# Routing sums in the second attention: GpSimd adds the two halves of each expert's products, VectorE sums 64 values in place of 128

## The chip, the cores and the metric

One core of one Trainium2 chip runs the whole network as one program. The metric is the device time of one execution in microseconds, the median of several runs.

## The reference

Two layers work on 64 x 64 tokens of 128 values (4096 tokens, 32 units of 128 tokens). Each layer has an attention over the tokens' own sequence and a context, and then a feed-forward part made of experts. What matters here is the second attention and the router of the second experts:

```python
normed = hidden_states * jax.lax.rsqrt(var + 1e-08) * norm_weight
flat = normed.reshape(-1, d)
probs = jax.nn.sigmoid(flat @ router_w.T)        # 8 experts
scores, idx = jax.lax.top_k(probs, TOPK)         # TOPK = 2
```

The product `flat @ router_w.T` is, for each token and each of the 8 experts, a sum of 128 products. The hidden states are the residual after the second attention.

## The kernel before

The program has four stages, one behind the other: `attention0` (to about 260 us), `experts`, `attention1` (from about 700 to 1180 us) and `sorted_experts`. The residual `x` stays in SBUF, 32 units of 128 tokens by 128 values.

`attention1` is a pipeline written out by hand. Each engine runs `for n in ticks` over 46 ticks, and in each tick it works on parts of several units that are at different steps: in tick n TensorE computes the scores of unit n, the values times probabilities of unit n - 2, the queries and keys of later pairs and the output projection of an earlier pair. The order within a tick is fixed on each engine by the list of calls at the end of its block, and all order between engines is by semaphores (`tally` objects, whose `at(k)` is the count after k steps).

Four units make a group. When the attention's output of a group has been normalised (`normalise_y`, L1752, VectorE), scaled and shifted by GpSimd (`scale_y`, L1302 and L1304) and added to the residual by VectorE (`add_up`, L1761), the routing of that group may start. The first five groups of eight (ROUTED = 5) are routed inside this stage, between the attention's own work, by `route_on_pool`, `route_on_act` and `route_on_dve`. `group_at(n, k)` is the group that is at its k-th routing tick in tick n; a group's routing starts every four ticks, and lasts eleven, so two or three groups overlap.

- In routing ticks 0 to 3 GpSimd multiplies one unit each (`multiply`, L1309): the unit's 128 values times the router's weights of each of the 8 experts, 8 x 128 products for each token, into one of two buffers `prod` (the profile calls them c_work, because they lie in a work tile).
- In routing ticks 2 and 4 VectorE sums two units each (`reduce`, L1796): 8 sums of 128 for each token into `raw`. `multiply(m)` waits until `reduce(m - 2)` is done, since it writes the same buffer.
- Then come logits (L1804 to L1807), the exponential on ScalarE, probabilities (L1812), a comparison of all experts with each other on GpSimd (L1317), ranks (L1820 to L1822), positions by TensorE, the choice of two (L1841), a payload that ScalarE fills (L1454) and eight scatters (L1324) that GpSimd issues.

The steps of the attention that the prediction speaks of: VectorE writes the low part of the normed and turned input (`x_lower`, L1661, c_x_lo), which TensorE's `values` of the next tick waits for; it copies the values out of PSUM (L1669, c_v); its reciprocal of the softmax sums (L1710) lets GpSimd scale the probabilities (L1292); ScalarE copies the turned probabilities out of PSUM (L1413, c_probT). GpSimd's order in a tick is `scale_y`, `scale` twice, `route_on_pool`, `split_context` (L1281 and L1284). VectorE's is the softmax's clip (L1683) and subtraction (L1690), `route_on_dve`, L1717, `add_up`, `normalise_y`, the sums (L1697), L1661 and so on.

Of the kernel before, what the change touches and what calls it, by code (L numbers as in the profile page):

```python
# [29 lines left out]
ALU = mybir.AluOpType  # L30
ACT = mybir.ActivationFunctionType
AX = mybir.AxisListType

P = 128
B, N, C = 64, 64, 128
UNITS = B * N // P
GROUP = 4
# [1056 lines left out]
def attention1(nc, earlier, x, stats, ident, a, route, dest_rows):  # L1094
# [8 lines left out]
    with stage(nc, earlier) as ctx:  # L1103
        def sb(name, shape, dt=F32):
            return ctx.enter_context(nc.sbuf_tensor("c_" + name, shape, dt))
# [4 lines left out]
        def sem(name):  # L1110
            return ctx.sem("c_" + name)

        def tally(name):
            return Tally(ctx, "c_" + name)
# [33 lines left out]
        prod = work[:, :].rearrange("p (s e c) -> p s e c", s=2, e=E)  # L1148
# [5 lines left out]
        raw, logit, expo = (sb(n, [P, GROUP, E]) for n in ("raw", "logit", "expo"))  # L1154
# [45 lines left out]
        for cc in range(CC):  # L1200
# [5 lines left out]
        tables = ((rw[:, :, :], a["d_rw_wide"]), (norm_wide, a["d_norm_wide"]),  # L1206
                  (sums_raw, a["sums"].rearrange("p n f -> p (n f)")), (route.before[:, :, :], a["before"]),
                  (route.first_row[:, :], a["first_row"]), (route.ids[:, :, :], a["ids"]))
        tables_in, rw_made, rw_summed, r_step, scattered = (sem(n) for n in ("tables_in", "rw_made", "rw_summed", "r_step",
                                                                             "scattered"))  # L1210
        r_var_done, r_root_done, r_scaled = tally("r_var"), tally("r_root"), tally("r_scaled")
        multiplied, reduced, logit_done, expo_done = (tally(n) for n in ("multiplied", "reduced", "logit", "expo"))
        prob_done, compared, masked, pos_done = (tally(n) for n in ("prob", "compared", "masked", "pos"))
# [55 lines left out]
        def _(pool):  # L1269
# [36 lines left out]
            def multiply(m):  # L1306
                pool.wait_ge(added_up.sem, added_up.at(m // GROUP + 1))
                pool.wait_ge(reduced.sem, reduced.at(m - 1))
                pool.tensor_tensor(prod[:, m % 2, :, :], x[:, m, :].unsqueeze(1).to_broadcast([P, E, C]), rw[:, :, :],  # L1309
                                   ALU.mult).then_inc(multiplied.sem, 1)  # L1310

            def compare(g):
                by_j = both[:, 0, :, :].unsqueeze(2).to_broadcast([P, GROUP, E, E])
# [13 lines left out]
            def route_on_pool(n):  # L1327
                if n == 0:
                    pool.wait_ge(tables_in, 16 * len(tables))
                    pool.tensor_tensor(rw[:, :, :], rw[:, :, :], norm_wide.unsqueeze(1).to_broadcast([P, E, C]), ALU.mult  # L1330
                                       ).then_inc(rw_made, 1)
                    pool.tensor_tensor(route.sums[:, :, :].rearrange("p n f -> p (n f)"), sums_raw,
                                       zero[:, 0:1].to_broadcast([P, 2 * P]), ALU.subtract).then_inc(rw_made, 1)
                    pool.wait_ge(rw_made, 2)
                    weights.wait(pool, len(jobs))
                for j in range(GROUP):
                    g = group_at(n, j)
                    if g is not None:
                        multiply(GROUP * g + j)
                g = group_at(n, 5)  # L1340
                if g is not None:
                    compare(g)
                for j, (lo, hi) in enumerate(((0, 3), (3, 6), (6, 2 * GROUP))):
                    g = group_at(n, 8 + j)
                    if g is not None:
                        scatter(g, lo, hi)
# [300 lines left out]
        def _(dve):  # L1647
# [145 lines left out]

            def reduce(m):
                dve.wait_ge(multiplied.sem, multiplied.at(m + 1))
                dve.tensor_reduce(raw[:, m % GROUP, :], prod[:, m % 2, :, :], AX.X, ALU.add).then_inc(reduced.sem, 1)  # L1796

            def logits(g):
                per_row = lambda t: t[:, g % 2, :].unsqueeze(2).to_broadcast([P, GROUP, E])
# [57 lines left out]
            def route_on_dve(n):  # L1857
                if n == 4:
                    dve.wait_ge(rw_made, 2)
                    dve.tensor_reduce(rw_sum[:, :], rw[:, :, :], AX.X, ALU.add).then_inc(rw_summed, 1)  # L1860
                g = group_at(n, 8)
                if g is not None:
                    place(g)
                g = group_at(n, 7)
                if g is not None:
                    pick(g)
                g = group_at(n, 6)
                if g is not None:
                    choose(g)
                g = group_at(n, 5)  # L1870
                if g is not None:
                    probabilities(g)
                g = group_at(n, 4)
                if g is not None:
                    reduce(GROUP * g + 2)
                    reduce(GROUP * g + 3)
                    logits(g)
                g = group_at(n, 2)
                if g is not None:
                    scales(g)  # L1880
                    reduce(GROUP * g)
                    reduce(GROUP * g + 1)
# [615 lines left out]
def program(nc, a, rows, gates, planes, out):  # L2498
    with ExitStack() as ctx:
        earlier = Earlier()  # L2500
        x = ctx.enter_context(nc.sbuf_tensor("x_resid", [P, UNITS, C], F32))
        stats = ctx.enter_context(nc.sbuf_tensor("x_stats", [P, UNITS, 6], F32))
        ident = ctx.enter_context(nc.sbuf_tensor("identity", [P, P], F32))
        headmask = ctx.enter_context(nc.sbuf_tensor("headmask", [P, FOUR], F32))
        attention0(nc, earlier, x, stats, ident, headmask, a["x"], a["a_wqkvT"], a["a_wprojT"], a["a_bproj"],
                   a["a_ctx_kT"], a["a_ctx_v"], a, rows)
        experts(nc, earlier, x, stats, ident, a, gates)
        route = Routing(nc, ctx)
        attention1(nc, earlier, x, stats, ident, a, route, rows)
        sorted_experts(nc, earlier, x, stats, ident, a, rows, planes, out, route)  # L2510
        with nc.Block() as block:
            @block.sync
            def _(sp):
                earlier.clear(sp)
        earlier.replace([], ExitStack())
# [79 lines left out]
```

## Time and profile before

| | |
|---|---|
| median of 3 runs | 1485.86 us (1478.29, 1485.86, 1489.66) |
| profiled execution | 1490.25 us, span 1488.4 us |
| granted TensorE clock, mean | 0.936 |
| TensorE busy | 1255.5 us, 84% |
| VectorE busy | 1056.2 us, 71% |
| ScalarE busy | 897.0 us, 60% |
| GpSimd busy | 650.9 us, 44% |

Busy time is a sum over stages with different limits, so it doesn't say what an edit in one stage is worth. An operation that stands because another engine holds what it needs is shown as busy for all that time. The end of idle time before an instruction is put down to the engine and line that released it ("<-"). "issue" is time in which the engine waited for nothing that the profile shows.

### The profile page before, as it was taken

The numbers are of one execution on the slowest core, as the hardware profiler recorded it, in microseconds if no ns is written. First come the engines' busy times: TensorE is split into PE (matmuls) and PEld (weight loads), VectorE is DVE, ScalarE is ACT, GpSimd is POOL, SyncE is SP. The second block draws the span as 40 slices with busy tenths as digits, with TensorE's granted clock in tenths as the row PEclk, the third lists the DMA queues.
The fourth block names the chain that finished last, engine by engine and source line by source line (L and its number), as shares of the span: only waits on it lengthen the run. The fifth ranks groups of instructions, "written<-read, shape, count | busy, mean of one in ns | idle before, by whom it ended". The sixth has DMA issues, their size and how long they took to land. (4 is left out here: it accounts for less than half of the span.)

```text
span 1488.4 us, 35941 instructions
## 1 busy us (share of the span) xinstructions
PE 1255.5 (84%) x13401; PEld 1043.8 (70%) x13401; DVE 1056.2 (71%) x2080; ACT 897.0 (60%) x1699; POOL 650.9 (44%) x677
## 2 busy tenths in 40 slices
PE   4999998399999999995799999998995269998970
PEld 3777776277777777783798888887885157786750
DVE  5888887576777677764456688898896377676652
ACT  3888887566666666654455565655653258777740
POOL 3222222155555555564423345566563335165551
PEclk9999999599999999997899999999999659999985
DMA  4222221333221322131200000000000122156626
GB/s 141 92 92 94 95 97 52 120 88 91 74 65 50 91 74 65 50 93 58 84 16 10 16 10 16 11 21 27 10 12 16 52 72 78 36 168 210 219 96 182
DMA packets 88373, 109.64 MB, mean 74 GB/s; under 512 B 13322, under 2 KB 55050, under 8 KB 88202
## 3 DMA queue, kind: packets, MB, share of 16 engines
q1 hardware_dynamic: 83210, 97.05, 20.8%
q0 software_dynamic: 4992, 10.30, 2.1%
q8 instruction: 109, 1.79, 0.5%
q14 instruction: 62, 0.51, 0.1%
HBM read 61.70 MB, written 29.82 MB: 61 GB/s over the span
## 5 line engine op out<-in xcount | busy, mean ns | idle before, releaser
L828 POOL TENSOR_TENSOR b_h_lo<-b_h,b_h_hi 128x512 fp32r<-128x512 f32 x168 | 216.5, 1293 | 179.0 <-ACT b_h_hi L852 178.6
L847 ACT ACTIVATE b_zg<-b_zg 128x512 f32<-128x512 f32 x168 | 97.7, 581 | 82.2 <-PE b_zg L892 81.8
L852 ACT ACTIVATE b_h_hi<-b_h 128x512 fp32r<-128x512 f32 x168 | 105.1, 626 | 65.3 <-DVE b_h L1057 65.3
L2171 POOL DMA_INDIRECT planes_dram<-d_y_out,d_back x92 | 93.8, 1020 | 110.8 <-DVE d_y_out L2474 85.3
L1057 DVE TENSOR_TENSOR b_h<-b_zg,b_uw 128x512 f32<-128x512 f32 x168 | 116.2, 692 | 32.0 <-ACT b_zg L847 26.7
L1050 DVE TENSOR_TENSOR b_uw<-b_zu,b_gw 128x512 f32<-128x512 f32 x128 | 88.2, 689 | 57.2 <-PE b_zu L892 51.0
L2443 DVE TENSOR_TENSOR d_h_lo<-d_h,d_h_hi 128x512 fp32r<-128x512 f32 x124 | 85.4, 695 | 53.0 <-ACT d_h_hi L2208 33.1
L312 POOL TENSOR_TENSOR a_qx<-a_qT,headmask 128x256 f32<-128x256 f32 x64 | 37.9, 612 | 149.1 <-ACT a_qT L347 149.1
L1292 POOL TENSOR_TENSOR c_prob<-c_prob,c_recip 128x512 f32<-128x512 f32 x64 | 65.5, 1044 | 59.8 <-DVE c_recip L1710 59.8
L519 DVE TENSOR_REDUCE a_top<-a_score_ps 128x8 f32<-128x1024 f32 x64 | 78.1, 1220 | 18.5 <-PE a_score_ps L410 18.5
L1717 DVE TENSOR_TENSOR c_oT_lo<-c_oy,c_oT_hi 128x512 fp32r<-128x512 f32 x64 | 43.7, 683 | 55.9 <-ACT c_oT_hi L1420 55.5
L1493 PE MATMUL c_p<-c_c_hi,c_wk_hi 128*128 128x256 f32 x256 | 76.8, 300 | 5.2 <-ACT c_qx L1385 4.4
L523 DVE TENSOR_TENSOR a_prob<-a_score_ps,a_top 128x1024 f32<-128x1024 f32 x64 | 78.4, 1224 | 2.2
L419 PE MATMUL a_probT_ps<-identity,a_prob 128*128 128x128 f32 x512 | 69.1, 279 | 10.3 <-ACT a_prob L336 10.3
L331 ACT ACTIVATE a_probT<-a_probT_ps 128x512 f32<-128x512 f32 x128 | 68.8, 589 | 12.8 <-PE a_probT_ps L419 12.8
L2208 ACT ACTIVATE d_h_hi<-d_h 128x512 fp32r<-128x512 f32 x124 | 75.3, 627 | 0.0
L890 PE MATMUL b_zu<-b_x_hi,b_w_hi 128*128 128x512 f32 x168 | 67.4, 401 | 6.9 <-DVE b_uw L1050 6.9
L1494 PE MATMUL c_p<-c_c_lo,c_wk_hi 128*128 128x256 f32 x256 | 73.0, 285 | 0.0
L1495 PE MATMUL c_p<-c_c_hi,c_wk_lo 128*128 128x256 f32 x256 | 73.0, 285 | 0.0
L1385 ACT ACTIVATE c_qx<-c_p 128x512 f32<-128x512 f32 x64 | 38.0, 596 | 54.7 <-PE c_p L1495 52.5
L336 ACT ACTIVATE a_prob<-a_prob 128x1024 f32<-128x1024 f32 x64 | 67.7, 1058 | 3.7 <-DVE a_prob L523 2.2
L890 PE MATMUL b_zg<-b_x_hi,b_w_hi 128*128 128x512 f32 x168 | 69.5, 413 | 0.0
(387 smaller groups left out, 4178.7 us busy)
## 6 DMA issues: line engine op xcount, KB each, us to landing
rows_dram<-a_blank SPq DMA_DIRECT2D x32, 520.0 KB, 3.2
b_gw<-gates_dram SPq DMA_DIRECT2D x64, 256.0 KB, 3.6
d_up_slot<-d_up_tab SPq DMA_DIRECT2D x15, 512.0 KB
d_down_slot<-d_down_tab SPq DMA_DIRECT2D x15, 512.0 KB
d_xg<-rows_dram SPq DMA_DIRECT2D x23, 260.0 KB
b_gm<-gates_dram SPq DMA_DIRECT2D x32, 160.0 KB, 3.7
c_craw<-in_c_ctxT_dram SPq DMA_DIRECT2D x16, 256.0 KB, 3.0
d_pay<-planes_dram SPq DMA_DIRECT2D x16, 256.0 KB, 4.7
```

The source lines that it names most:

```text
L519: dve.tensor_reduce(by_band(top[:, b, :]), score_ps[:, :, b, :, :], AX.X, ALU.max).then_inc(max_done.sem, 1)
L523: dve.tensor_tensor(prob[:, b, :, :].rearrange("p (i t) k -> p i t k", t=2), score_ps[:, :, b, :, :], by_band(top[:, b, :]).unsqueeze(3).t ...
L828: pool.tensor_tensor(h_lo[:, m % HS, :], h[:, m % HF, :], h_hi[:, m % HS, :].bitcast(F32), ALU.subtract).then_inc(lo_done.sem, 1)
L847: act.activation(zg_ps[:, n % ZG, :], zg_ps[:, n % ZG, :], ACT.Silu).then_inc(sg_done.sem, 1)
L852: act.activation(h_hi[:, m % HS, :], h[:, m % HF, :], ACT.Copy).then_inc(hi_done.sem, 1)
L890: pe.matmul(dst, hi, m_hi, start=start, stop=False)
L1050: dve.tensor_tensor(uw[:, n % 2, :], zu_ps[:, n % ZU, :], gate_tile(s), ALU.mult).then_inc(weighed.sem, 1)
L1057: dve.tensor_tensor(h[:, n % HF, :], zg_ps[:, n % ZG, :], uw[:, n % 2, :], ALU.mult).then_inc(h_done.sem, 1)
L1493: pe.matmul(dst, hi, m_hi, start=start, stop=False)
L2171: pool.indirect_dma_start(planes, bass.IndirectOffsetOnAxis(ap=back[:, t, u:u + 1], axis=0), y_out[:, t % 2, u, :], None).then_inc(added[t ...
L2208: act.activation(h_hi[:, q % HS, :], h[:, q % HF, :], ACT.Copy).then_inc(hi_done.sem, 1)
L2443: dve.tensor_tensor(h_lo[:, q % HS, :], h[:, q % HF, :], h_hi[:, q % HS, :].bitcast(F32), ALU.subtract).then_inc(lo_done.sem, 1)
```

## The change

In `multiply` the product now signals a new semaphore `halved`, GpSimd waits for it itself, and then adds the second half (values 64 to 127) of each expert's products to the first half, in place. Only this add signals `multiplied`, on which VectorE waits. `reduce` sums the first 64 values of each expert in place of 128. Nothing else changes; the order of the calls, the buffers and the other engines' work are the same. Twenty units go through this (five groups of four).

```diff
-        tables_in, rw_made, rw_summed, r_step, scattered = (sem(n) for n in ("tables_in", "rw_made", "rw_summed", "r_step",
-                                                                             "scattered"))
+        tables_in, rw_made, rw_summed, r_step, scattered, halved = (sem(n) for n in (
+            "tables_in", "rw_made", "rw_summed", "r_step", "scattered", "halved"))
...
                 pool.wait_ge(added_up.sem, added_up.at(m // GROUP + 1))
                 pool.wait_ge(reduced.sem, reduced.at(m - 1))
                 pool.tensor_tensor(prod[:, m % 2, :, :], x[:, m, :].unsqueeze(1).to_broadcast([P, E, C]), rw[:, :, :],
-                                   ALU.mult).then_inc(multiplied.sem, 1)
+                                   ALU.mult).then_inc(halved, 1)
+                pool.wait_ge(halved, m + 1)
+                pool.tensor_tensor(prod[:, m % 2, :, 0:C // 2], prod[:, m % 2, :, 0:C // 2], prod[:, m % 2, :, C // 2:], ALU.add
+                                   ).then_inc(multiplied.sem, 1)
...
             def reduce(m):
                 dve.wait_ge(multiplied.sem, multiplied.at(m + 1))
-                dve.tensor_reduce(raw[:, m % GROUP, :], prod[:, m % 2, :, :], AX.X, ALU.add).then_inc(reduced.sem, 1)
+                dve.tensor_reduce(raw[:, m % GROUP, :], prod[:, m % 2, :, 0:C // 2], AX.X, ALU.add).then_inc(reduced.sem, 1)
```

## Rows read from the trace of the kernel before

**Rows 1.** Windows, before routing and with it: busy us and number by engine, TensorE's clock

```profile
731.00:851.00 120.00, 117.39 (x1850) 104.51 (x1851) 76.12 (x132) 67.67 (x123) 39.42 (x45) 1.00 0.07 22
851.00:1125.00 274.00, 255.69 (x4037) 227.56 (x4036) 231.22 (x467) 159.92 (x303) 151.93 (x136) 0.99 0.05 15
```

**Rows 2.** Timeline of TensorE: start us, us, instruction [idle before <-releaser]

```profile
901.25 0.69 PE L1587 MATMUL c_oy<-c_probT,c_v 64*64 64x64 f32 x32 [1.33 <-DVE c_x_lo L1661]
...
954.40 1.14 PE L1587 MATMUL c_oy<-c_probT,c_v 64*64 64x64 f32 x32 [2.08 <-ACT c_probT L1413]
...
1010.26 0.69 PE L1587 MATMUL c_oy<-c_probT,c_v 64*64 64x64 f32 x32 [2.09 <-ACT c_probT L1413]
```

**Rows 3.** Groups by line, 840 to 1150 us, GpSimd and VectorE: busy us, mean ns

```profile
L1292 POOL TENSOR_TENSOR c_prob<-c_prob,c_recip 128x512 f32<-128x512 f32 x48 | 49.1, 1044 | 38.0 <-DVE c_recip L1710 38.0
L1309 POOL TENSOR_TENSOR c_work<-x_resid,c_rw 128x1024 f32<-128x1024 f32 x20 | 47.7, 2386 | 43.3 <-DVE c_raw L1796 43.3
...
L1304 POOL TENSOR_TENSOR c_y_sb<-c_y_sb,c_ln_b 128x512 f32<-128x512 f32 x6 | 7.8, 1302 | 0.5
...
L1796 DVE TENSOR_REDUCE c_raw<-c_work 128x8 f32<-128x1024 f32 x20 | 23.4, 1210 | 0.0
...
L1822 DVE TENSOR_REDUCE c_rank<-c_gt 128x32 f32<-128x256 f32 x5 | 2.1, 421 | 0.2
```

**Rows 4.** Timeline of GpSimd in a tick with a group's fourth multiply

```profile
1000.83 2.39 POOL L1309 TENSOR_TENSOR c_work<-x_resid,c_rw 128x1024 f32<-128x1024 f32 x1
...
1004.57 1.29 POOL L1302 TENSOR_TENSOR c_y_sb<-c_y_sb,c_ln_w 128x512 f32<-128x512 f32 x1
1005.94 1.28 POOL L1304 TENSOR_TENSOR c_y_sb<-c_y_sb,c_ln_b 128x512 f32<-128x512 f32 x1
```

**Rows 5.** Timeline of VectorE behind L1304, in the first group and in the third

```profile
898.97 0.69 DVE L1761 TENSOR_TENSOR x_resid<-x_resid,c_y_sb 128x512 f32<-128x512 f32 x1 [3.03 <-POOL c_y_sb L1304]
...
900.71 0.28 DVE L1661 TENSOR_TENSOR c_x_lo<-c_oy,c_x_hi 128x128 fp32r<-128x128 f32 x1
...
1007.26 0.69 DVE L1761 TENSOR_TENSOR x_resid<-x_resid,c_y_sb 128x512 f32<-128x512 f32 x1 [2.33 <-POOL c_y_sb L1304]
...
1009.00 0.28 DVE L1661 TENSOR_TENSOR c_x_lo<-c_oy,c_x_hi 128x128 fp32r<-128x128 f32 x1
```

**Rows 6.** Timelines of GpSimd and VectorE around the two L1841

```profile
944.95 2.39 POOL L1309 TENSOR_TENSOR c_work<-x_resid,c_rw 128x1024 f32<-128x1024 f32 x1
947.29 0.62 POOL L1281 TENSOR_TENSOR c_c_hi<-c_craw,c_zero 128x256 fp32r<-128x256 f32 x1
...
946.20 1.22 DVE L1841 SCALAR_TENSOR_TENSOR c_chosen<-c_rank,c_both 128x64 f32<-128x64 f32 x1
...
947.35 0.65 DVE L1841 SCALAR_TENSOR_TENSOR c_chosen<-c_rank,c_both 128x64 f32<-128x64 f32 x1
```

**Rows 7.** Timelines of VectorE and GpSimd in a tick with a group's first sums

```profile
989.98 2.34 DVE L1796 TENSOR_REDUCE c_raw<-c_work 128x8 f32<-128x1024 f32 x2
...
993.04 1.55 DVE L1752 TENSOR_SCALAR c_y_sb<-c_y_sb,c_y_agg,c_y_rstd 128x128 f32<-128x128 f32 x4
...
998.29 0.63 DVE L1669 TENSOR_TENSOR c_v<-c_p,c_nv 128x512 f32<-128x512 f32 x1
...
991.34 2.40 POOL L1309 TENSOR_TENSOR c_work<-x_resid,c_rw 128x1024 f32<-128x1024 f32 x1 [5.01 <-DVE c_raw L1796]
```

**Rows 8.** Timeline of VectorE behind a group's last sums, third group, and at the end

```profile
1022.25 0.29 DVE L1661 TENSOR_TENSOR c_x_lo<-c_oy,c_x_hi 128x128 fp32r<-128x128 f32 x1 [0.92 <-ACT c_x_hi L1378]
...
1128.63 0.69 DVE L1717 TENSOR_TENSOR c_oT_lo<-c_oy,c_oT_hi 128x512 fp32r<-128x512 f32 x1 [2.40 <-ACT c_oT_hi L1420]
```

**Rows 9.** Windows and timeline of TensorE behind the waits at 954 and 1010 us

```profile
954.00:958.00 4.00, 3.60 (x101) 3.49 (x102) 2.26 (x6) 1.42 (x3) 2.04 (x2) 0.57 0.02 4
...
957.55 0.35 PE L1494 MATMUL c_p<-c_x_lo,c_wq_hi 128*128 128x256 f32 x1
...
1012.04 0.28 PE L1494 MATMUL c_p<-c_x_lo,c_wq_hi 128*128 128x256 f32 x1
```

## The prediction

> **What bounds the kernel now.** The windows view was read first, to find the stage and its bound. The second attention's full pace runs from 731 to 851 us without routing and from 851 to 1125 us with it. In the first stretch TensorE is busy 117.4 of 120 us, in the second 255.7 of 274 us, both at practically full clock, while VectorE is at 231.2 and GpSimd at 151.9 of 274 [rows 1]. So TensorE sets the pace. It waits 18.3 us in the routed stretch, and a change there pays or costs only through those waits. The timeline of TensorE gives them: 1.33 us at 901.25 until VectorE had written c_x_lo, then once in each later group of four ticks some 2.08 us until ScalarE had copied c_probT [rows 2]. Two of them stand there, 954.40 in the second group and 1010.26 in the third; the fourth group repeats the third.
>
> The groups view gives the prices, and the timelines of GpSimd and VectorE around the waits say what is late. A group has four ticks of about 14 us (1010.26 - 954.40, over four [rows 2]). GpSimd multiplies one unit a tick. VectorE sums two units in each of two of the four ticks.
>
> **Step 1, VectorE is relieved, but not where anyone waits.** Twenty sums over 1024 elements take 1210 ns each; the same operation over 256 takes 421 ns [rows 3]. On the straight line between them (1.027 ns an element) 512 elements cost 684 ns, so 526 ns less each, 10.5 us over twenty. The bounds are 421 ns, a sum of half the size again, and 1210 ns, if the input with gaps (64 read, 64 skipped) is no faster; the rows lie on one line of element count, so I take 684. Where do the 10.5 us go? In one of the two ticks VectorE comes, after the sums and the logits, to the x_lo at L1661 and waits 0.92 us there for ScalarE [rows 8]; that wait grows by what the sums save. The very last sums are followed, up to 1128.63, by a wait of 2.40 us for ScalarE [rows 8]. In the other tick the 1.05 us of two sums are spent in step 3. So I take 0 us of gain, with 10.5 us as the far bound, where every saved nanosecond lies on the path.
>
> **Step 2, GpSimd is later with the layer norm of the attention.** Each multiply gets an add of 128x512 behind it. The nearest rows are L1304, also two full inputs of 128x512 in place, 1302 ns, and L1292, whose second input is one value for each 64, 1044 ns [rows 3]. I take 1.29 us, L1304 as it runs in the timeline (1.28), and 0.08 us from the end of L1302 to the start of L1304 (1004.57 + 1.29 to 1005.94) for the wait on the semaphore [rows 4]: 1.37 us, twenty times 27 us. The bounds are 1.12 and 1.48 (1.40, the slowest L1304, plus 0.08). In three of the four ticks GpSimd has the room: it idles 5.01 us before the multiply at 991.34 alone [rows 7]. The wait on `halved` holds up everything behind it on GpSimd; the scatters of 0.96 us go 1.37 us later, and the payload they read isn't rewritten before the next group's tick 6.
>
> The tick with the group's fourth multiply is full: multiply at 1000.83, two context splits, L1302 at 1004.57, L1304 from 1005.94 to 1007.22, nothing idle between [rows 4]. VectorE has already waited 2.33 us when it starts L1761 at 1007.26, and its sums, c_x_lo (done 1009.28) and c_v follow without a gap [rows 5]. So all of it comes 1.37 us later. In the first group TensorE's wait ends by that very c_x_lo (901.25, 0.25 us after its end at 901.00) [rows 2, 5]: 1.37 us, full. In groups 2 to 4 TensorE starts at 1010.26 by ScalarE's c_probT, and c_x_lo with its 0.25 us would have allowed 1009.53: 0.73 us of cover. What is left is 0.64 us, three times 1.9 us. The fifth instance has no c_x_lo any more (all units' inputs are turned by then); between 0 and 1.37 I take 0.3 us for it. Step 2: 1.37 + 1.9 + 0.3 = 3.6 us; with the bounds of the add 2.6 to 4.0.
>
> **Step 3, VectorE is held at the port.** The first L1841 starts at 946.20 and lasts 1220 ns, to 947.42, just behind the end of a multiply at 947.34; the second, started 947.35, lasts 0.65, to 948.00, just behind the end of L1281 at 947.90 [rows 6]. An operation of VectorE that reads SBUF twice stands while GpSimd works, and GpSimd's next instruction gets in between two of VectorE's. The Trainium skill's page SBUF — State Buffer, section "SBUF: two separate sides", says the same: VectorE and GpSimd share a port pair that one holds for a whole instruction while the other "fully blocks". By that rule the add is one more such block, and this trace agrees, with the two ends above.
>
> Applied to the other tick of the sums: the multiply at 991.34 waits on the first sum [rows 7]. With a sum of 0.68 us it starts at 990.8 and ends at 993.2, the add runs 993.3 to 994.6. Of the four L1752 the first begins at 993.04 now and stands until the multiply ends (991.34 + 2.40 = 993.74), the last ends at 994.59, 0.85 us after that. With the change they begin at 992.0. The first is held to 993.2, the second by the add to 994.6, and with three of four left (0.64 us) the last ends about 995.2: 0.6 us later in spite of the shorter sums. From there VectorE has no gap until c_v at 998.29 [rows 7], and the reciprocal just ahead of it lets GpSimd scale, so that the next tick's full row of GpSimd starts later too, by an estimated 0.5 of the 0.6 us. That adds 0.5 us to the lateness of step 2 in groups 2, 3 and 4: 1.5 us. For the first group I take nothing, since its L1752 comes after a wait for ScalarE, and nothing for the last, which has the cover of step 2. If VectorE wins the port after the multiply, step 3 is 0; if L1841, now held by the add as well, delays L1717 beyond TensorE's need of it, 0.4 us more in each, 2.7 us.
>
> **Sum.** 0 + 3.6 + 1.5 = 5.1 us, between 2.6 and 6.7. What follows starts behind the stage's end, so it moves with it. The profiled execution took 1490.25 us (span 1488.4); it would be 1495.4. The median of the runs shown is 4.4 us under it: 1485.86 + 5.1 = 1491.0 us.
>
> **Rivals.** *The relief counts after all.* VectorE at 231 of 274 us is close to being a second bound, and if the ticks were set by its total and not by single waits, up to 10.5 us would come back: 1485.9 - 10.5 = 1475.4 us. It decides only where VectorE, not ScalarE or GpSimd, is what others wait for; against it stands the wait of 0.92 us right behind the sums [rows 8].
>
> *Nothing moves.* If the semaphore and the add are hidden in all groups but the first, or the waits on ScalarE take everything in, the sum is 0 to 1.4 us: 1486 us. Only 0.64 us a group stand against that.
>
> *The clock falls with the longer waits.* After the wait at 954.40 the granted clock was 0.57 in 954 to 958, half speed for most of it [rows 9]. From the end of the wait to the second query matmul took 3.15 us there (957.55 - 954.40) and 1.78 after the like wait at 1010.26 (1012.04): 1.37 us lost. One of three such waits did it. If the four lengthened waits all do, 5.5 us come on top: 1496.5 us.
>
> A rule against the change stands in the Trainium skill's GPSIMD Engine Reference, section "4.1 Engine selection": elementwise work with two inputs belongs on VectorE, about twice as fast there. No row here has the same add on VectorE, and the rule wouldn't alter the sum, since the bound is who waits.
>
> **How the numbers follow.** Chances: as forecast 0.5, clock 0.15, nothing moves 0.2, relief counts 0.12, something else 0.03. The three runs of before alone spread from 1478.3 to 1489.7, so a per cent (14.9 us) is about what can be told from no change. The range takes the forecast, the clock case and no change with that spread: 1479 to 1502 us. Faster by over 1% (under 1471) would need more than the whole relief, 0.03; slower by over 1% (over 1500.7) needs the clock case and more, 0.07; within 1% 0.90.
>
> **What would show it.** Step 1: L1796 at about 0.68 us, and VectorE's waits before L1661 and at 1128 longer. Step 2: adds near 1.29 us, L1761 waiting about 3.7 us, TensorE's wait at 901 about 2.7 us and those of groups 2 to 4 ended by c_x_lo at about 3.2. Step 3: L1752 in a group above 1.56 us in sum, L1841 above 1.79. Wrong would be the whole if TensorE's waits in the routed stretch sum to less than 18.3 us, or if the stage's first wait is no longer.

## The result, and the profile after

The changed kernel takes 1491.76 us (median of 20 runs, 1479.68 to 1498.91) against 1486.24 us for the kernel before (20 runs, 1478.29 to 1490.93). The ratio is 1.004, interval 1.0024 to 1.0056: 3.6 to 8.3 us slower, well inside one per cent. The profiled execution has a span of 1484.6 us, *shorter* than the one of before (1488.4), and must not be read as a gain. The last L1304 of the second attention starts at 1177.64 us in it, and at 1174.12 before, 3.5 us later; what lies between that instruction and the end took 307.0 us here and 314.3 us before. The last stage, which the change does not touch, differs by 7.3 us between these two executions, more than the change is worth. So the reading below is of the stage alone.

The windows of the two stretches of [rows 1], same columns:

```profile
731.00:851.00 120.00, 118.19 (x1860) 105.46 (x1861) 77.22 (x133) 68.15 (x124) 40.61 (x46) 1.00 0.07 22
851.00:1125.00 274.00, 252.84 (x3977) 224.10 (x3976) 231.57 (x457) 159.01 (x302) 175.65 (x154) 0.99 0.05 15
```

GpSimd has 23.7 us more, in 18 more instructions (the twenty adds are 25.9 us in the groups below). But VectorE, whose sums were halved, is at 231.57 us, where it was at 231.22 [rows 1]. The groups by line of the same stretch (840 to 1150 us) say why, first those of after, then the lines of before that answer to them (L1796 of before is in [rows 3]). In after's file a line of VectorE stands 3 lower.

```profile
L1309 POOL TENSOR_TENSOR c_work<-x_resid,c_rw 128x1024 f32<-128x1024 f32 x20 | 47.7, 2386 | 35.4 <-DVE c_raw L1799 35.4
L1312 POOL TENSOR_TENSOR c_work<-c_work 128x512 f32<-128x512 f32 x20 | 25.9, 1293 | 1.6
...
L1686 DVE TENSOR_SCALAR c_top<-c_top 128x16 f32<-128x16 f32 x23 | 23.1, 1006 | 0.8
L1799 DVE TENSOR_REDUCE c_raw<-c_work 128x8 f32<-128x512 f32 x20 | 12.7, 677 | 0.0
L1755 DVE TENSOR_SCALAR c_y_sb<-c_y_sb,c_y_agg,c_y_rstd 128x128 f32<-128x128 f32 x20 | 11.0, 611 | 0.2
L1807 DVE TENSOR_TENSOR c_raw<-c_raw,c_r_rstd 128x32 f32<-128x32 f32 x5 | 8.0, 1606 | 0.2
L1810 DVE TENSOR_TENSOR c_logit<-c_logit,c_raw 128x32 f32<-128x32 f32 x5 | 5.2, 1034 | 0.2
...
L1844 DVE SCALAR_TENSOR_TENSOR c_chosen<-c_rank,c_both 128x64 f32<-128x64 f32 x8 | 3.9, 530 | 0.0
```

```profile
L1683 DVE TENSOR_SCALAR c_top<-c_top 128x16 f32<-128x16 f32 x23 | 17.1, 745 | 0.8
L1752 DVE TENSOR_SCALAR c_y_sb<-c_y_sb,c_y_agg,c_y_rstd 128x128 f32<-128x128 f32 x20 | 7.4, 429 | 0.2
L1804 DVE TENSOR_TENSOR c_raw<-c_raw,c_r_rstd 128x32 f32<-128x32 f32 x5 | 5.8, 1168 | 0.2
L1841 DVE SCALAR_TENSOR_TENSOR c_chosen<-c_rank,c_both 128x64 f32<-128x64 f32 x8 | 5.7, 754 | 0.0
...
L1807 DVE TENSOR_TENSOR c_logit<-c_logit,c_raw 128x32 f32<-128x32 f32 x5 | 1.0, 195 | 0.2
```

The sums went from 23.4 to 12.7 us: 10.7 us less. The same instructions as before, with the same inputs, take longer: the clip c_top 6.0 us more, L1755 3.6, L1807 2.2, L1810 4.2. That is 16.0 us, and L1844 gives 1.8 back. These are not more work but holds: such an instruction of VectorE stands until GpSimd's instruction has ended, and is shown as busy (the rows under steps 2 and 3 below have the ends of both side by side). The relief was paid back in holds (the total stays level although they exceed it, because the slower pipeline has 457 instructions of VectorE in the window for 467).

The timeline of TensorE has the waits before the values, with those of [rows 2] as their counterparts (before, the waits ended by c_y_sb did not exist):

```profile
901.50 0.69 PE L1590 MATMUL c_oy<-c_probT,c_v 64*64 64x64 f32 x32 [2.69 <-DVE c_x_lo L1664]
941.90 0.69 PE L1590 MATMUL c_oy<-c_probT,c_v 64*64 64x64 f32 x32 [0.47 <-DVE c_y_sb L1734]
955.44 0.69 PE L1590 MATMUL c_oy<-c_probT,c_v 64*64 64x64 f32 x32 [2.31 <-DVE c_x_lo L1664]
...
997.41 0.69 PE L1590 MATMUL c_oy<-c_probT,c_v 64*64 64x64 f32 x32 [0.49 <-DVE c_y_sb L1734]
1010.95 0.69 PE L1590 MATMUL c_oy<-c_probT,c_v 64*64 64x64 f32 x32 [2.33 <-DVE c_x_lo L1664]
```

A wait of 0.5 us is new in groups 2 to 4, and the long waits of these groups changed their releaser. In group 5 the same place (1109.76 us) has some of its matmul records missing, so its wait can't be read in this trace. From the start of the first multiply to the end of the fifth long wait (the "stretch" from here on; 849.91 to 1121.82 us here) it is 271.91 us, and 267.08 before: 4.8 us more. Group by group the long waits lie 1.36, 0.79, -0.35, 2.60 and 0.43 us further apart. The third and fourth number differ by where a fall of TensorE's granted clock lay (third group before, fourth after; each execution has one between these waits). At the 1.37 us worked out for it in the prediction they become 1.02 and 1.23. TensorE's waits in this trace add up to 3.3 us more than before over the stretch; the other 1.5 us of the 4.8, among them the wait of group 5, it doesn't show.

### The profile page after: what moved, and what is told of

It is laid out like the page before. It is cut to its first block and busy times, and to the rows that moved or that the text cites. A ratio compares the mean times of both kernels' runs of the same rounds, so it can differ in the third digit from the quotient of the medians.

```text
span 1484.6 us, 35962 instructions
## 1 busy us (share of the span) xinstructions
PE 1251.9 (84%) x13401; PEld 1039.3 (70%) x13401; DVE 1060.7 (71%) x2080; ACT 897.7 (60%) x1699; POOL 675.8 (46%) x697
## 3 DMA queue, kind: packets, MB, share of 16 engines
q8 instruction: 109, 1.79, 0.5%
## 5 line engine op out<-in xcount | busy, mean ns | idle before, releaser
L828 POOL TENSOR_TENSOR b_h_lo<-b_h,b_h_hi 128x512 fp32r<-128x512 f32 x168 | 216.5, 1293 | 179.2 <-ACT b_h_hi L852 178.8
L1292 POOL TENSOR_TENSOR c_prob<-c_prob,c_recip 128x512 f32<-128x512 f32 x64 | 65.4, 1044 | 58.7 <-DVE c_recip L1713 58.7
L1423 ACT ACTIVATE c_oT_hi<-c_oy 128x512 fp32r<-128x512 f32 x64 | 38.3, 598 | 54.8 <-PE c_oy L1590 47.2
```

Source lines behind the costliest of these rows:

```text
L828: pool.tensor_tensor(h_lo[:, m % HS, :], h[:, m % HF, :], h_hi[:, m % HS, :].bitcast(F32), ALU.subtract).then_inc(lo_done.sem, 1)
```

## Experiments

All comparisons are with the kernel before on the same chip. These chips run it in about 1465 us, some 20 us less than the first one, with the exception of the last run's (1478 us); so ratios and stretches are compared. A ratio always has the kernel before on the same chip beside it. A stretch is that of one execution, and some of the pairs below ran on two different chips. Two runs set the scale: the two kernels again, unchanged.

**The kernel before, unchanged.**

> The kernel before, unchanged, for its trace on the chip of the experiments. All theories expect no difference in time (within 2 us). What it tells: how many of TensorE's long waits are followed by a fall of the clock here. If falls are as frequent as in the trace shown (one of three), the three falls in the run of the short sums alone cost that run some 3 us; if all three waits are followed by one here too, they don't.

Ratio 1.0006 (0.9995 to 1.0017), stretch 266.59 us.

**The changed kernel, unchanged.**

> The changed kernel, unchanged, on the chip of the experiments. Expected: the ratio of 1.004 again (5 to 6 us slower), from the start of the first multiply to TensorE's fifth long wait 4 to 5 us longer than in the kernel before, the same places (1.36 us in the first group, about 1 us in groups 2 to 4).

Ratio 1.002 (1.0008 to 1.0032), 2.9 us; stretch 269.80 us, 3.2 us more. TensorE's waits account for it: 0.46, 0.67, 0.67 and 0.59 us before c_y_sb are new, 2.4 us in all; the long ones of groups 1 to 4 are 2.69, 2.42, 2.32 and 2.31 where they were 1.32 and three times 2.08, 2.2 us in all. That is 4.6 us (TensorE's waits for c_v are 0.2 us shorter in sum). The rest is the clock. These are windows of TensorE's columns (PE busy, weights, VectorE, ScalarE, GpSimd, then the granted clock), first of the kernel before, then of the changed one:

```profile
950.00:960.00 10.00, 7.92 (x128) 6.99 (x127) 7.10 (x15) 6.16 (x16) 3.81 (x4) 0.83 0.09 28
1010.00:1020.00 10.00, 10.00 (x179) 9.68 (x169) 7.96 (x15) 3.50 (x7) 5.10 (x4) 0.83 0.02 3
1060.00:1070.00 10.00, 7.92 (x129) 7.04 (x129) 7.33 (x17) 6.11 (x14) 3.33 (x3) 0.83 0.02 4
```

```profile
900.00:910.00 10.00, 7.67 (x135) 7.58 (x136) 9.68 (x14) 1.80 (x4) 4.32 (x4) 0.83 0.02 4
...
1010.00:1020.00 10.00, 7.68 (x142) 7.08 (x141) 8.36 (x18) 5.80 (x14) 3.69 (x4) 1.00 0.09 29
1060.00:1070.00 10.00, 7.69 (x141) 6.55 (x135) 7.40 (x15) 7.78 (x18) 6.67 (x8) 1.00 0.01 2
```

Before, the clock fell after each of the three 2.08 us waits, where in the first profile it fell after one of them. In the changed kernel it fell at 900 and between 950 and 970 and not after the last two. Two falls for three: 1.4 us back, and 4.6 - 1.4 = 3.2 us, as measured. One execution each, so the falls are noise of plus or minus one or two, not an effect of the change.

**The relief alone.** The kernel before; only the sum is shortened. Half of the products are left out, so other experts are chosen. The ratio takes in the stage that works with this choice, so the stretch is the better evidence here.

```diff
-                dve.tensor_reduce(raw[:, m % GROUP, :], prod[:, m % 2, :, :], AX.X, ALU.add).then_inc(reduced.sem, 1)
+                dve.tensor_reduce(raw[:, m % GROUP, :], prod[:, m % 2, :, 0:C // 2], AX.X, ALU.add).then_inc(reduced.sem, 1)
```

> VectorE sums 64 of the 128 products, GpSimd adds nothing (half of each routing sum is left out, so experts are chosen by half a logit). This is the relief alone. Measured on the stage, from the start of the first multiply to the end of the last L1302 (323.0 us before, 327.7 after). My theory (VectorE's relief lies where it waits for ScalarE or is spent): 322 to 323 us, the whole within 2 us of before. Rival (the relief counts where VectorE is busy 231 of 274 us): 312 to 318 us, the whole 5 to 10 us faster.

Ratio 1.0013 (1.0004 to 1.0023), stretch 266.30 us, all long waits as before (1.32, three times 2.08, 1.21). The groups of VectorE:

```profile
L1796 DVE TENSOR_REDUCE c_raw<-c_work 128x8 f32<-128x512 f32 x20 | 12.7, 675 | 0.0
...
L1804 DVE TENSOR_TENSOR c_raw<-c_raw,c_r_rstd 128x32 f32<-128x32 f32 x5 | 8.1, 1610 | 0.2
L1841 DVE SCALAR_TENSOR_TENSOR c_chosen<-c_rank,c_both 128x64 f32<-128x64 f32 x8 | 6.8, 893 | 0.0
```

10.7 us less work on VectorE moves the stretch by 0.3 us. (The ratio has it 1.9 us slower; that stays open.) Even without the add, 2.3 us of it went into L1804 (5.8 before): VectorE comes there sooner and stands longer behind the multiply that its own first sum has released.

**The add alone.** The changed kernel, with the sum left at 128 columns. The upper half then counts twice, so here too other experts are chosen.

```diff
-                dve.tensor_reduce(raw[:, m % GROUP, :], prod[:, m % 2, :, 0:C // 2], AX.X, ALU.add).then_inc(reduced.sem, 1)
+                dve.tensor_reduce(raw[:, m % GROUP, :], prod[:, m % 2, :, :], AX.X, ALU.add).then_inc(reduced.sem, 1)
```

> The add on GpSimd is kept, VectorE sums all 128 again (the upper half counts twice in the logits). If the add alone makes the loss, through GpSimd's full row in front of L1304: 327 to 328 us for the stage, like after. If the relief of VectorE pays part of it back (the four L1752/L1755 come 1.05 us earlier): 329 to 331 us. If the loss came from the shorter sums (multiplies that start earlier and hold VectorE at other places), it is gone: 323 us.

Ratio 1.0028 (1.0017 to 1.0039), stretch 272.27 us. TensorE waits 1.00, 1.21, 1.20 and 1.13 us for c_y_sb where the changed kernel waits 2.4 us in sum: 2.1 us more. So the relief, worth nothing alone, seems to be worth some 2 us beside the add, by these waits of one execution each: it gives back part of the lateness that the add makes. The ratios have 1.2 us, but their intervals overlap, so they can't tell it from nothing.

**The add twice.** A second add of the same size behind the first.

```diff
...
+                pool.wait_ge(halved, 2 * m + 2)
+                pool.tensor_tensor(prod[:, m % 2, :, C // 2:], prod[:, m % 2, :, C // 2:], prod[:, m % 2, :, C // 2:], ALU.add
+                                   ).then_inc(multiplied.sem, 1)
```

> A second add of 128x512 behind the first (on the upper half, which nobody reads afterwards), with its own wait: GpSimd's row is 1.37 us longer once more in each of 20 ticks. If the loss is the lateness of L1304 behind the multiply of the same tick, with the cover of 0.73 us in groups 2 to 4 already used up, each of the first four groups costs the full 1.37 us more: stage 327.7 + 5.5 = 333 us, and the long waits of TensorE are ended by c_x_lo at 4.0 us (group 1) and 3.7 us. If the loss is only in port holds, VectorE is held once more in each group but L1304's lateness costs nothing: 328 to 330 us.

Ratio 1.0121 (1.0103 to 1.0139), 18 us, more than expected; stretch 283.88 us, 14.1 above the changed kernel's. It is 17.3 us over the kernel before, where one add has 3.2: more than five times the loss for twice the adds. VectorE's groups and TensorE's waits:

```profile
L1758 DVE TENSOR_SCALAR c_y_sb<-c_y_sb,c_y_agg,c_y_rstd 128x128 f32<-128x128 f32 x20 | 17.0, 908 | 0.2
L1767 DVE TENSOR_TENSOR x_resid<-x_resid,c_y_sb 128x512 f32<-128x512 f32 x6 | 4.2, 692 | 19.8 <-POOL c_y_sb L1304 19.8
...
1005.98 0.69 PE L1593 MATMUL c_oy<-c_probT,c_v 64*64 64x64 f32 x32 [1.96 <-DVE c_y_sb L1737]
1020.53 0.84 PE L1593 MATMUL c_oy<-c_probT,c_v 64*64 64x64 f32 x32 [2.41 <-DVE c_x_lo L1667]
```

The waits for c_y_sb are 1.3 to 2.0 us now, and the clock fell in seven places between 900 and 1130 us, after these waits too. That makes the clock rival real at this size: five falls more than the two of the changed kernel are some 7 us of the 14.

**The layer norm's scale and shift first.** GpSimd's L1302 and L1304 one tick's order earlier, ahead of the multiply of that tick, in the changed kernel and in the kernel before.

```diff
-                scale_y(n - 7)
                 scale(n - 1, 0)
                 scale(n - 1, 1)
+                scale_y(n - 6)
```

> The changed kernel with scale_y (L1302, L1304) moved one tick forward, between scale and multiply, so that it no longer stands behind multiply and add. If step 2 is right, L1764 waits for L1304 no more, c_x_lo no longer ends the long waits, the first group's wait (2.69 us) goes and the others fall back to ScalarE's 2.08 us: stage 322 to 324 us, the whole as fast as before or 1 to 2 us faster. If the loss is in the port holds instead, the stage stays at 326 to 328 us.

> The kernel before with scale_y (L1302, L1304) one tick earlier, between scale and multiply. The first group's wait of 1.33 us for c_x_lo goes; groups 2 to 4 wait for ScalarE's c_probT as before, so there only VectorE gains. My theory: 1 to 2 us faster than before, and 1.5 us (step 3) faster than the changed kernel with the same move. Rival (the port): L1302 and L1304 now hold VectorE's L1841 and L1761 at other places, and the gain is taken back: no difference.

Changed kernel: ratio 1.0007 (0.9997 to 1.0018), stretch 266.81 us. Kernel before: ratio 0.9996 (0.9986 to 1.0006), stretch 263.86 us. In both the wait of group 1 is gone. In the changed kernel there remain, for one group:

```profile
996.68 0.69 PE L1590 MATMUL c_oy<-c_probT,c_v 64*64 64x64 f32 x32 [0.68 <-DVE c_y_sb L1734]
1006.24 0.30 PE L1505 MATMUL c_oy<-identity,c_xn 128*128 128x128 f32 x1 [0.55 <-DVE c_oT_lo L1720]
1010.46 0.69 PE L1590 MATMUL c_oy<-c_probT,c_v 64*64 64x64 f32 x32 [2.08 <-ACT c_probT L1416]
```

The last one is in the kernel before as well. The first two kinds are not in its counterpart: 0.46, 0.68, 0.67 and 0.61 us for c_y_sb, 0.77, 0.55 and 0.58 for c_oT_lo, 4.3 us. Less one fall of the clock (one here, two in its counterpart) that is the 2.95 us between the two stretches. The ratios are 1.6 us apart, with intervals that overlap a little. So with no wait of TensorE left that the layer norm's lateness ends, the changed kernel still waits 4.3 us more, and all of it for VectorE. But only part of that is VectorE held by an add: the waits for c_y_sb stand behind L1755, which the add holds as in step 3 below. The waits for c_oT_lo stand behind the two L1844, and those are held by the old multiply. The rows are first of the changed kernel, then of its counterpart:

```profile
1002.46 2.59 DVE L1844 SCALAR_TENSOR_TENSOR c_chosen<-c_rank,c_both 128x64 f32<-128x64 f32 x2
...
997.54 0.35 DVE L1841 SCALAR_TENSOR_TENSOR c_chosen<-c_rank,c_both 128x64 f32<-128x64 f32 x2
```

The multiply runs from 1002.56 to 1004.96 in the first, and starts only at 998.99, behind both L1841, in the second. VectorE comes late there because L1302 held its clip just before (1.10 us in place of 0.23). Later by one hold, it runs into the next.

**The add at the end of the tick**, behind the context splits L1281 and L1284.

```diff
...
                 split_context(n + 4)
+                for j in range(GROUP):
+                    if group_at(n, j) is not None:
+                        halve(GROUP * group_at(n, j) + j)
```

> The changed kernel with the add moved to the end of GpSimd's tick, behind the context splits, in place of right behind the multiply. L1304 of the fourth tick still stands behind the add (scale_y opens the next tick), so step 2 is unchanged (3.6 us); step 3 falls away where the add held L1755: TensorE's waits of 0.47 us for c_y_sb in groups 2 to 4 go or shrink. Expected 3 to 4 us over before, 1 to 2 us under the changed kernel. If instead the place right behind the multiply is the whole trouble: no difference to before.

Ratio 1.0083 (1.0069 to 1.0097), 12 us: a miss. GpSimd's timeline, and one instruction of VectorE:

```profile
977.26 0.61 POOL L1281 TENSOR_TENSOR c_c_hi<-c_craw,c_zero 128x256 fp32r<-128x256 f32 x1 [2.86 <-issue]
977.95 0.73 POOL L1284 TENSOR_TENSOR c_c_lo<-c_craw,c_c_hi 128x256 fp32r<-128x256 f32 x1
978.64 1.27 POOL L1314 TENSOR_TENSOR c_work<-c_work 128x512 f32<-128x512 f32 x1
980.60 2.05 POOL L1292 TENSOR_TENSOR c_prob<-c_prob,c_recip 128x512 f32<-128x512 f32 x2 [0.68 <-DVE c_recip L1718]
...
979.12 0.82 DVE L1792 TENSOR_SCALAR c_r_tmp<-c_r_agg 128x4 f32<-128x4 f32 x1
```

L1281 itself comes late, 2.86 us after GpSimd was free. The add that could have filled this gap now starts behind it. There it holds VectorE's L1792 until it ends (979.91): 0.82 us, where it was 0.17 in the changed kernel, in each of the five groups. L1792 lies ahead of the copy of c_v, and TensorE's wait for c_v went from 0.7 to 1.0 us to 1.62 in each of the groups. In the tick ahead of a group's fourth multiply the add (1005.79 to 1007.08) lies right in front of the next tick's first work: L1292 starts at 1007.04, though c_recip was there at 1006.15, and the multiply, L1302 and L1304 come later with it. The long waits of groups 2 to 4 went from 2.3 to between 3.3 and 3.6. Right behind the multiply was the better place.

**ScalarE's payload in two parts.** To see what the 2.08 us waits are worth once their first cause is gone: the fill of L1454, 3.18 us in one piece ahead of the copies c_probT, half in routing tick 6, half in 7. The kernel before with this; with the layer norm first as well; and the changed kernel with both.

```diff
-            def fill(g):
+            def fill(g, part):
...
-                for u in range(GROUP):
+                for u in range(part * GROUP // 2, (part + 1) * GROUP // 2):
...
+                if group_at(n, 7) is not None:
+                    fill(group_at(n, 7), 1)
```

> The kernel before, with ScalarE's eight c_pay activations of a group (3.18 us in one piece, right ahead of the copies of the turned probabilities) cut into two fours, in two following ticks. In the unchanged kernel TensorE waits 2.08 us for those copies in groups 2 to 4. Theory 1 (that wait is set by ScalarE's order and each microsecond of it counts): the three waits fall by up to 1.6 us each, until the next cause ends them (the LayerNorm chain, some 0.5 us earlier or later than ScalarE's copies in the trace of before); stretch from the first multiply to the fifth long wait 2 to 4 us shorter (266.6 to 263 or 264.5), time ratio 0.997 to 0.999, and the fall of the granted clock behind each of the three waits is gone if the wait itself is what brings it. Theory 2 (the two causes end within 0.3 us of each other, so one alone moves nothing): the waits stay at about 2 us, now ended by VectorE's c_x_lo, ratio 1.000. Theory 2 has 0.6.

> The kernel before with both edits: GpSimd's scale and shift of the output rows one tick earlier, ahead of the multiply, and ScalarE's c_pay in two fours. Both causes of the 2.08 us waits are then out of the way. Theory 1 (the waits are serial cost): waits of groups 2 to 4 at 0.7 us or less, the wait of group 1 gone as in the version with the one edit, stretch 260 to 262.5 us against 266.6, ratio 0.995 to 0.998, a version that is faster than both kernels. Theory 2 (VectorE's wait for GpSimd's c_y_sb merely moves to other ticks, and ScalarE's second half delays something else): ratio 0.999 to 1.001, and new short waits at c_oT_lo or c_v of 0.6 us. Theory 1 has 0.6.

> The changed kernel with the same two edits. If the change costs through GpSimd's queue in front of the LayerNorm alone, it now costs nothing and this equals the kernel before with both edits (ratio 0.995 to 0.998, stretch within 1 us of that one's). If the holds of VectorE (the longer c_top, c_y_sb and c_logit instructions while GpSimd adds) count too, now that the waits which hid them are gone, it is 0.3 us a multiply tick or 3 to 6 us above that one (ratio 0.999 to 1.001). The second has 0.6: with the one edit the changed kernel was 3 us above the kernel before with the same edit.

Ratios 1.0171 (1.015 to 1.0192), 1.015 (1.0132 to 1.0169) and 1.0181 (1.016 to 1.0201). All three are 21 to 25 us slower by their medians, and the expectations failed in sign. The 2.08 us wait did fall, to 1.3 us and with both edits to 0.54, but a larger one came. VectorE's and TensorE's timelines of the second kernel:

```profile
1022.51 0.17 DVE L1852 CAST c_dest<-c_pair 128x8 int32<-128x8 f32 x1 [7.85 <-ACT c_pay L1454]
...
1027.97 0.45 PE L1505 MATMUL c_oy<-identity,c_xn 128*128 128x128 f32 x1 [6.45 <-DVE c_oT_lo L1720]
```

VectorE waits for the filled payload in routing tick 7, early in its order; ScalarE's second half is late in its own. Everything behind on VectorE waits 7.85 us, and TensorE behind that 6.5 us. Nobody had waited for that semaphore before, so no view of the trace showed it; the code did. The pair of kernels with both edits still tells one thing: changed against not changed, 1491.41 against 1488.05 us, 3.4 us on the same chip. The change costs about the same in this surrounding too.

**GpSimd's time without the add.** The kernel before, with three writes of zeros behind each multiply.

```diff
...
+                for i in range(3):
+                    if m or i:
+                        pool.wait_ge(halved, 3 * m + i)
+                    pool.memset(spare[:, :], 0.0).then_inc(halved, 1)
```

> The kernel before, its sums over 128 columns as they were, with three writes of zeros by GpSimd (128x400 each, into a buffer that nothing reads) right behind each multiply, where the change has its add. From the two zero writes at the start of the program (128x520 in 0.53 us, 128x4096 in 3.51) three of them take about 1.3 us with the gaps, as the add does: GpSimd's queue is as long as in the changed kernel, but no add reads SBUF. What is not known and will be seen first: whether a VectorE instruction that lies beside such a write is held (mean of c_y_sb L1755 611 ns in the changed kernel and 371 in the kernel before; c_top 1006 and 745). If it is not held, the two prices of the change come apart. Theory 1 (the queue in front of the LayerNorm is the larger part): the wait of group 1 at 2.6 to 2.7 us, waits of groups 2 to 4 at 2.3 ended by c_x_lo, no c_y_sb waits; stretch 269 to 270 us against 266.6, ratio 1.0015 to 1.0025. Theory 2 (the holds are the larger part, as the two kernels with the LayerNorm first suggest, still 2.95 us apart): stretch 267 to 268.5, ratio 1.000 to 1.001. Theory 2 has 0.6. If the writes hold VectorE as the add does, the result is that of the version with the add and sums over 128: 1.003.

Ratio 1.0058 (1.0034 to 1.0082), stretch 276.51 us. The three writes took 1.41 us with their gaps, 0.1 us more than meant. VectorE's timelines in a tick with the group's fourth multiply, and in one with its second:

```profile
1006.32 0.22 DVE L1688 TENSOR_SCALAR c_top<-c_top 128x16 f32<-128x16 f32 x1
...
1014.24 0.69 DVE L1766 TENSOR_TENSOR x_resid<-x_resid,c_y_sb 128x512 f32<-128x512 f32 x1 [4.12 <-POOL c_y_sb L1305]
...
979.66 2.56 DVE L1688 TENSOR_SCALAR c_top<-c_top 128x16 f32<-128x16 f32 x1
```

The first two lines show the lateness of step 2 of the prediction on VectorE: nothing holds it in this tick, so it comes early and waits for the late L1305, 4.12 us where it was 2.33 [rows 5]. The third shows that the experiment is not as clean as meant: the clip stands not only until the multiply ends (981.81) but 0.4 us more, to 982.22, the length of one write of zeros; so a write holds VectorE too, and TensorE's wait for c_xn grew from 0.18 to 0.55 us in each group. The long waits are 2.66, 2.67, 2.55 and 2.56 us (the last three ended by ScalarE's c_probT, so not by that lateness), 2.9 us more in sum, c_xn makes 1.8 and two more falls of the clock 2.7 than the first profile of before. Of 9.4 us that is 7.4; the rest stays open. The forecast of the run (ratio 1.000 to 1.001, at 0.6) was a miss. But since the writes hold VectorE too, the run can't part queue from hold: what queue time costs by itself stays open.

## Why the prediction was right, and where its steps were not

**The sum held, in part by luck.** 5.1 us was forecast (1491.0 us), 5.5 measured (1491.76 - 1486.24), 4.8 in the profiled stretch; the measured time lies in the range, and the change is a loss of well under one per cent as forecast. But two of its parts were off, in opposite directions (step 2 by 1.4 us too dear, step 3 by 0.9 us too cheap, in the traces of the second pair), and the same two kernels on the second chip are only 2.9 us apart (1.2 to 4.7).

**Step 1, the relief taken at 0, held, with a remark.** The sum took 677 ns (684 forecast) and the relief alone moved nothing. But where its time would go was only half seen. VectorE's wait before L1664 hardly grew (1.00 us, 0.92 before [rows 8]); the wait at the end grew by 1.0 us, to 3.41; the rest became holds, of instructions that the prediction did not name: L1807 (1606 ns for 1168) and L1810 (1034 for 195), which stand behind the multiply and then the add that VectorE's own first sum has released. And beside the add the relief may be worth some 2 us by the waits, which the step gave as zero.

**Step 2 was right in the first group and too dear after it.** The adds take 1293 ns, and L1304 ends 7.75 us after the fourth multiply starts where it was 6.39: 1.36 us. In group 1 TensorE's wait is 2.69 us, where 2.7 was forecast. In groups 2 to 4 it is 2.3, where 3.2 was forecast, and VectorE's wait at L1764 did not grow at all:

```profile
1001.10 2.19 DVE L1686 TENSOR_SCALAR c_top<-c_top 128x16 f32<-128x16 f32 x1
...
1008.67 0.69 DVE L1764 TENSOR_TENSOR x_resid<-x_resid,c_y_sb 128x512 f32<-128x512 f32 x1 [2.34 <-POOL c_y_sb L1304]
...
1000.88 2.39 POOL L1309 TENSOR_TENSOR c_work<-x_resid,c_rw 128x1024 f32<-128x1024 f32 x1
1003.35 1.29 POOL L1312 TENSOR_TENSOR c_work<-c_work 128x512 f32<-128x512 f32 x1
```

These are VectorE and GpSimd in the third group's tick with the fourth multiply. The clip came 0.2 us too late: it starts behind the multiply's start and stands until it has ended, 2.19 us, where it had slipped in ahead in 0.23 us before. That hold is not in the prediction. It costs nothing, because it lies ahead of the very wait that was to grow; the run with zeros, where the clip kept its place (0.22 us), shows the wait at 4.12.

Why TensorE's wait is 2.3 and not 3.2 us is in the distances from the start of the fourth multiply. TensorE may start by c_x_lo 10.07 us after it (1010.95 - 1000.88), where 8.70 would have done before: 1.37 us later, as forecast. But TensorE itself comes to the wait 7.74 us after it, where it came 7.34 after it before: it is 0.4 us later too, by its own wait for c_y_sb a tick ahead. With the cover of 0.73 us, 0.24 us are left of the 1.37. The prediction had added 0.5 us of step 3 here, which should have been taken off.

**Step 3 was right in kind and too small.** Same group, tick of the first sums:

```profile
989.61 1.27 DVE L1799 TENSOR_REDUCE c_raw<-c_work 128x8 f32<-128x512 f32 x2
...
992.33 2.47 DVE L1755 TENSOR_SCALAR c_y_sb<-c_y_sb,c_y_agg,c_y_rstd 128x128 f32<-128x128 f32 x4
994.72 1.21 DVE L1700 TENSOR_REDUCE c_total<-c_prob 128x16 f32<-128x1024 f32 x1
990.44 2.39 POOL L1309 TENSOR_TENSOR c_work<-x_resid,c_rw 128x1024 f32<-128x1024 f32 x1 [4.48 <-DVE c_raw L1799]
992.91 1.29 POOL L1312 TENSOR_TENSOR c_work<-c_work 128x512 f32<-128x512 f32 x1
```

The four L1755 are held by the multiply until 992.83 and by the add until 994.20, as worked out. The last ends 5.19 us after the sums' start, 4.61 before [rows 7]: 0.58 us later, where 0.6 was forecast. What the step missed is who sees it. It passed the lateness on through GpSimd's next tick; but a few instructions further, still in the same tick, VectorE copies c_y_sb (L1734, 996.74 to 997.15), and TensorE's values wait for that first. So it has a wait of its own, 0.46 to 0.67 us in each of four groups, not three: the last group, which the prediction gave nothing, has it as well.

Put side by side, in the pair of traces on one chip: step 2 (the long waits) 2.2 us for 3.6 forecast, step 3 (the waits for c_y_sb) 2.4 us for 1.5, together 4.6 for 5.1. The two share the waits rather than stack up, as the kernel with the layer norm first also shows: step 2 gone, and 4.3 us of waits still there, part of them now before c_oT_lo.

**The rivals.** That the relief counts is refuted by the run with the relief alone. That nothing moves is refuted by the ratio and by the waits. The clock is the noise of one execution here (one fall for one, two for three), but with the add doubled it is seven falls, and about half of the loss.

**Two signs in "what would show it" were wrong**: L1764's wait (2.34, not 3.7) and L1841's sum, which was to rise above 1.79 us and is 0.81 in this tick, since the held clip ahead of it moved it out of the multiply's way.

**No version here beats the kernel before** by a margin that is measured: the layer norm first in it gave 0.9996 (0.9986 to 1.0006).

## What to carry to other kernels

Moving part of a sum from a busy engine to an idle one pays only if someone waits for the busy one, and where both reach for the same port the idle engine's instruction comes back as holds: compare the busy time of untouched lines, not only of the edited one. Follow a delay to the first reader, not along the engine on which it arose, and expect two delays in front of one wait to overlap rather than add. Before splitting or moving a producer, look in the code for every wait on its semaphore: a wait that has never waited is in no trace.

## What the runs showed of the hardware

- Holds depend on a race of some tenths of a microsecond. The same clip takes 0.23 us if it starts ahead of GpSimd's multiply, and 2.19 us if it starts 0.2 us behind. The clips' total of 17.1 us became 23.1 with not one clip more.
- What is held differs by instruction. L1755 and c_top (one SBUF input), c_logit and c_chosen (two) stood until GpSimd's instruction ended; the sums over SBUF did not (675 to 677 ns in every kernel with the short sum, also where the second of a pair ran beside a multiply).
- Three writes of zeros by GpSimd, which read nothing, held a clip for the length of one write (0.4 us), but left the two-input c_logit at 192 ns, which the add had brought to 1034. The Trainium skill's page SBUF — State Buffer, section "SBUF: two separate sides", makes this very distinction: a VectorE instruction with two SBUF inputs is blocked only by a GpSimd instruction that reads SBUF, one in a two-port mode by any. These traces agree as far as they go (1034 against 192 ns for the two-input c_logit); in which mode the clip ran, no run here shows.
- Sums over 64 of each 128 values take 677 ns for 512 read, on the line of the dense ones (1210 for 1024, 421 for 256): the gaps cost nothing.
- The granted clock fell to half (1.2 in place of 2.4 GHz) for some 3 us (0.83 in a window of 10 us) after one of three like waits of 2.08 us in one execution of the kernel before, and after three of three in another. Per execution that is 1.4 us each way, as large as a quarter of the change.
